# Attention bias by a plain load on the SP queue, masked by GpSimd additions, in place of a mask copy and an accumulating DMA

## What is computed

```python
scores = jnp.einsum('bhqd,bhkd->bhqk', q / math.sqrt(HEAD_DIM), k)
scores = scores + attention_bias
scores = jnp.where(src_mask, -jnp.inf, scores.astype(jnp.float32))
probs = jax.nn.softmax(scores, axis=-1).astype(v.dtype)
ctx = jnp.einsum('bhqk,bhkd->bhqd', probs, v)
```

## Time and profile before

| | |
|---|---|
| median of 3 runs | 686.55 us (685.88 to 686.61) |
| the profiled execution | 685.88 us, of which its span is 684.1 us |
| TensorE busy | 556.1 us, 81% |
| VectorE busy | 468.2 us, 68% |
| ScalarE busy | 296.7 us, 43% |
| GpSimd busy | 227.6 us, 33% |
| DMA | 86.50 MB, mean 126 GB/s |
| mean granted TensorE clock | 0.900 |

### The profile page before, as it was taken

The page is one execution under the profiler, slowest core; times in us unless marked ns, Lnnn a source line. Parts: engine busy times, 40 slices in busy tenths (PEclk is TensorE's granted clock), DMA queues, the critical chain, the costliest instruction groups (busy, mean ns, idle before and its releaser), DMA issues.

```text
span 684.1 us, 15743 instructions
## 1 busy us (share of the span) xinstructions
PE 556.1 (81%) x5032; PEld 415.9 (61%) x5033; DVE 468.2 (68%) x1300; ACT 296.7 (43%) x608; POOL 227.6 (33%) x137
## 2 busy tenths in 40 slices
PE   2719566999697998779948399999899999999992
PEld 0606255658385485764837248776676778777871
DVE  5574796589979979983798844886554656474751
ACT  1615542651564425525243141766564344353540
POOL 0412543207714338133280331212442223132222
PEclk9558768999989898979988689999999999999996
DMA  8583451913065452466606585782632322222220
GB/s 287 127 209 125 157 159 57 226 34 124 0 168 156 141 177 71 132 147 208 200 24 229 188 291 216 273 284 41 162 69 39 52 40 41 34 49 37 44 42 0
DMA packets 41177, 86.50 MB, mean 126 GB/s; under 512 B 7321, under 2 KB 31810, under 8 KB 37026
## 3 DMA queue, kind: packets, MB, share of 16 engines
q1 hardware_dynamic: 21744, 56.77, 24.3%
q0 software_dynamic: 8352, 16.99, 13.5%
q10 hardware_dynamic: 11026, 12.02, 5.9%
HBM read 57.23 MB, written 29.44 MB: 127 GB/s over the span
## 4 chain that ended last, share of the span: by engine, by line
PE 52%; DVE 25%; issue 6%; DMA 5%; ACT 5%; ACTq 3%; POOL 2%; SPq 0%; DVEq 0%; POOLq 0%
PE bank L1914 8%; PE bank L1903 5%; PE bank L1739 4%; PE bank L1905 4%; PE bank L1748 4%; PE bank L1904 4%; PE bank L1915 4%; DMA stage<-in_moe_w 4%; PE bank L1636 3%; PE bank L1703 3%; ACTq L850 2%; PE bank L1719 2%; PE bank L1654 2%; PE bank L1693 2%; DVE stats L1033 2%
## 5 line engine op out<-in xcount | busy, mean ns | idle before, releaser
L1903 PE MATMUL bank<-xs_f,w_moe 128*128 128x128 f16 x624 | 123.2, 221 | 13.0 <-ACT stage L862 6.0
L1905 PE MATMUL bank<-xs_f,w_moe 128*128 128x128 f16 x624 | 123.3, 221 | 0.0
L862 ACT ACTIVATE stage<-bank,cols 128x128 f32<-128x128 f32 x312 | 88.9, 374 | 78.7 <-PE bank L1905 35.2
L1904 PE MATMUL bank<-xs_f,w_moe 128*128 128x128 f16 x624 | 122.7, 220 | 0.0
L642 POOL DMA_INDIRECT out_x<-x_kept,ids x39 | 63.1, 1619 | 165.6 <-DVE x_kept L1505 102.3
L1903 PEld LDWEIGHTS bank<-xs_f,w_moe 128*128 x624 | 61.1, 98 | 49.9 <-issue 21.7
L1914 PE MATMUL bank<-w_moe,split 128*128 x208 | 79.3, 383 | 0.6
L1904 PEld LDWEIGHTS bank<-xs_f,w_moe 128*128 x624 | 61.4, 98 | 2.8
L1000 DVE SCALAR_TENSOR_TENSOR split<-stage,split 128x2048 f16<-128x2048 f32 x16 | 41.2, 2572 | 31.7 <-ACT split L681 31.7
L1739 PE MATMUL bank<-w_moe 128*128 128x512 f32 x128 | 59.8, 627 | 3.3 <-ACT w_moe L740 3.3
L1905 PEld LDWEIGHTS bank<-xs_f,w_moe 128*128 x624 | 61.2, 98 | 1.1 <-issue 0.2
(11 more groups left out here) (273 smaller groups left out, 1173.6 us busy)
## 6 DMA issues: line engine op xcount, KB each, us to landing
stage<-in_moe_w SPq DMA_DIRECT2D x16, 1024.0 KB, 8.6
w_split<-split SPq DMA_DIRECT2D x16, 1024.0 KB, 4.9
w_moe<-w_split SPq DMA_DIRECT2D x8, 2048.0 KB, 8.5
w_moe<-in_bias POOLq DMA_DIRECT2D x8, 1024.0 KB, 11.2
xs<-dispatched ACTq DMA_DIRECT2D x41, 130.0 KB
w_moe<-in_x_f SPq DMA_DIRECT2D x4, 512.0 KB, 6.8
w_moe<-in_x_t SPq DMA_DIRECT2D x4, 512.0 KB, 7.6
out_x<-x4b ACTq DMA_DIRECT2D x4, 512.0 KB, 3.6
```

Source lines behind the costliest of these rows:

```text
L862: ins = act.activation(h32[j][:, f, :], bank[banks + g][:, P * (f % 4):P * (f % 4) + P], ACT.Relu, bias=moe_b1[:, bass.ds(e, 1), f], scale ...
L1903: pe.matmul(o, hi, xs_f[j][:, k, :], start=(k == 0), stop=False)
L1904: pe.matmul(o, hi, xs_f[j][:, KD + k, :], start=False, stop=False)
L1905: mm = pe.matmul(o, lo, xs_f[j][:, k, :], start=False, stop=(k == KD - 1))
```

## The change

The bias no longer comes by an accumulating DMA on GpSimd's queue but by a plain load of the same 1 MB for each half, on SP's queue (`load_bias`). It waits only for the buffer to be free. The mask is no longer copied by ScalarE: GpSimd adds `mask_add` to the loaded bias in place, in four additions of 128x512 for each half, each of which VectorE waits for before it adds the scores of that part. The semaphore `mask_written` (one count a half) becomes `bias_masked` (four counts). GpSimd's `mask(c + 1)` stands behind `residual(c)`, ahead of `confirm(c)`; that of chunk 0 stands where `add_bias(0)` was. ScalarE's eight copies a chunk go.

```diff
@@ sync
+            def load_bias(c):
+                for u in range(2):
+                    sp.wait_ge(prob_turned[u].sem, prob_turned[u].of(c, 0))
+                    sp.dma_start(sc[u][:].rearrange("p r a h k -> p (r a h k)"),
+                                 t["bias"][bass.ds(c * 2 + u, 1), :, :].rearrange("s p n -> (s p) n")
+                                 ).then_inc(bias_in[u].sem, 16)
...
             load_x(0)
+            load_bias(0)
             load_x(1)
...
             load_tokens(2)
             for c in range(NCH - 1):
+                load_bias(c + 1)
                 store_part(c, 3)
                 load_part(c + 1, 0)
@@ gpsimd
-            def add_bias(c):
+            def mask(c):
                 for u in range(2):
-                    pool.wait_ge(mask_written[u].sem, mask_written[u].of(c, 1))
-                    pool.dma_start(sc[u][:].rearrange("p r a h k -> p (r a h k)"),
-                                   t["bias"][bass.ds(c * 2 + u, 1), :, :].rearrange("s p n -> (s p) n"),
-                                   accum_op=ALU.add).then_inc(bias_in[u].sem, 16)
+                    pool.wait_ge(bias_in[u].sem, bias_in[u].of(c, 16))
+                    for r in BANK_ORDER:
+                        pool.tensor_tensor(
+                            sc[u][:, r], sc[u][:, r],
+                            mask_add[:, bass.ds(c * TT + 2 * u, 2), :].unsqueeze(2).broadcast_to([P, 2, 4, S]),
+                            ALU.add).then_inc(bias_masked[u].sem, 1)
...
             pool.tensor_scalar(mask_add[:], mask_u8[:], MASKED, None, ALU.mult).then_inc(mask_ready, 1)
-            add_bias(0)
+            pool.wait_ge(mask_ready, 1)
+            mask(0)
...
             pool.wait_ge(main_in, N_MAIN)
-            add_bias(1)
             select(2)
             for c in range(NCH - 1):
                 residual(c)
+                mask(c + 1)
                 confirm(c)
                 less_maximum(c + 1, 0)
...
-                if c + 2 < NCH:
-                    add_bias(c + 2)
                 dispatch(c, range(TT))
@@ scalar
-            def mask(c, u):
-                act.wait_ge(prob_turned[u].sem, prob_turned[u].of(c, 0))
-                for r in range(4):
-                    ins = act.activation(sc[u][:, r],
-                                         mask_add[:, bass.ds(c * TT + 2 * u, 2), :].unsqueeze(2).broadcast_to([P, 2, 4, S]),
-                                         ACT.Copy)
-                ins.then_inc(mask_written[u].sem, 1)
...
             context(0, 0)
-            mask(1, 0)
             context(0, 1)
-            mask(1, 1)
             split_high(0, 3)
@@ vector
                         dve.wait_ge(score_done[u].sem, score_done[u].of(c, i + 1))
-                        if i == 0:
-                            dve.wait_ge(bias_in[u].sem, bias_in[u].of(c, 16))
+                        dve.wait_ge(bias_masked[u].sem, bias_masked[u].of(c, i + 1))
```

More of the change, by code:

```diff
@@ L351, in build @@
         v_done, v0_ready, v1_ready = free("v_done", 2), count("v0_ready", 2), count("v1_ready", 2)
-        mask_written = [count(f"mask_written{u}", 1) for u in range(2)]
+        bias_masked = [count(f"bias_masked{u}", 4) for u in range(2)]
         score_done = [count(f"score_done{u}", 4) for u in range(2)]
@@ L792, in _ @@
             act.activation(soft[:, 3], soft[:, 2], ACT.Ln).then_inc(setup_act, 1)
-            act.wait_ge(mask_ready, 1)
-            for u in range(2):
-                mask(0, u)
             act.wait_ge(main_in, N_MAIN)
@@ L835, in _ @@
                 context(c + 1, 1)
-                if c + 2 < NCH:
-                    for u in range(2):
-                        mask(c + 2, u)
                 split_high(c + 1, 2)
```

## The result

The changed kernel takes 699.63 us (median of 4 runs, 696.46 to 700.35), the kernel before 686.21 us beside it (685.84 to 686.61): ratio 1.0183, 95% interval 1.0164 to 1.0203. It is slower by 13.4 us; 9.25 were forecast.

A forecast was written before the change was run, and what follows sets the result against it. No engine was taken as the bound throughout; the chain in order of time was read. -2.1 + 0.9 + 2.05 + 5.6 + 2.8 = +9.25 on 686.55 gave 695.8 us; range 689 to 701, own case 692 to 699.

The forecast's parts named there:

- signs of being wrong: An addition of other than 1.0 us, Newton steps at 0.17 us throughout, or chunk 3's stage part landing in 8 us.
- Copies, -2.1: At 96.7 us, ScalarE's four mask copies ahead of `context(0, 1)` leave the chain: 2.1 us less.
- Chunk 0, +0.9: Additions run from 29.3 to 37.6 us; one falls under VectorE's Newton steps from 36.59 us: 0.9 us more.
- The stage load of chunk 0, +2.05: Near 50 us, an earlier stage part lets `split_low(0, 0)` between the two `shift_norm(0)` additions: 2.05 us more.
- Chunk 1, nothing: Additions at about 128 to 137 us run while VectorE idles or reads PSUM: no cost.
- Chunk 2, +5.6: Additions from 234.0 to 242.3 us hold seven of VectorE's nine Newton steps in chunk 3's norms: 5.6 us more.
- Chunk 3, +2.8: From 310.4 us chunk 3's bias on SP's queue delays the weight store and load behind it: 2.8 us more.
- the second pair starts 2.8 us later: `store_part(2, 3)` and `load_part(3, 0)`, issued at about 323 us, wait for 2 MB of bias moving at 280 GB/s until 326.2.
- hidden additions: Rival, chance 0.13: chunk 2's bias lands so that the norms are not hit; without the 5.6, 690.2 us.
- faster: Rival, chance 0.07: VectorE isn't held, the queue has room, the four copies at 96.7 us decide: -2.1 us, 684.5 us.
- Sharing: Rival, chance 0.10: the bias slows the weight part ahead of it, 7.3 instead of 2.8 us at 310 us: 700.3 us.
- A dear addition: Rival, chance 0.08: the broadcast makes each GpSimd addition cost 2 us instead of 1.04: 704 us.

The follow-up runs named there:

- again: The changed kernel measured and profiled a second time, no edit: 698.43 us, ratio 1.0187 to the kernel before.
- split0: The changed kernel, with VectorE made to wait for both additions of `shift_norm(0)` before `split_low(0, 0)`: 696.8 us, ratio 1.0163.
- noadd2: The changed kernel without the eight mask additions of chunk 2, loads as in the changed kernel: 689.9 us, ratio 1.0057.
- noadd: The changed kernel without any of the 32 mask additions, loads still on SP's queue: 685.13 us, ratio 0.9999.
- placed: The changed kernel with additions of chunks 0 and 2 moved, biases of chunks 2 and 3 loaded sooner, `split_low(0, 0)` behind both `shift_norm(0)` additions: 685.46 us, ratio 0.9993.
- bias3early: The changed kernel with chunk 3's bias loaded one weight part sooner, ahead of `store_part(2, 2)`: 700.88 us, ratio 1.0216.
- eight: The kernel before plus eight GpSimd additions of 128x512 into dead memory behind `residual(1)`, loads and copies untouched: 695.09 us, ratio 1.0133.
- maskmove: The kernel before with ScalarE's four mask copies `mask(1, 0)` moved behind `context(0, 1)`: 681.56 us, ratio 0.9933; second measurement 681.2 us, 0.9939.
- placed3: The kernel placed, with the second half of chunk 3's additions moved behind the weight part's `split_low(2, 3)`: 680.1 us, ratio 0.9932.

## Why the prediction was right or wrong

The direction was right, and the time, 699.63, lies within the range of 689 to 701, but it is 3.8 us above the forecast and outside the 692 to 699 that the prediction gave its own case. Two of its own signs of being wrong came: an addition took 1.26 us, and the stage part at chunk 3 landed in 8.00. Term by term, from the traces of after and again:

- **Copies, -2.1: right place, too small.** Measured 3.6 to 3.9 us in the changed kernel (from the maximum of (0,0) to `split_low(0,3)`: +3.3 to -0.6, +4.4 to +0.8). The chain's 2.07 us is only the idleness; the lower clock that this idleness left behind was another 1.5. The forecast never asked what TensorE's clock did behind a gap, although the 4.40 us of its 64 matmuls stood in the trace of before.
- **Chunk 0, +0.9: mechanism right, too small.** It was 2.0 us in after and in again (whose +2.4 at this point has 0.4 from before the additions). An addition takes 1.26 us instead of 1.04, so that the last ends at 39.1 instead of 37.6 us, and two steps are held instead of one (the next step starts at 40.35, before at 38.38).
- **The stage load of chunk 0, +2.05: right to the tenth.** 4.09 instead of 2.04 us for the pair, and split0 takes it away.
- **Chunk 1, nothing: right.** The additions run from 126.2 to 136.1 us in after; it is 0.6 us ahead of before at `split_low(0,3)` and 0.7 at the first scores of the chunk.
- **Chunk 2, +5.6: place, time and mechanism right, too small.** Its first half landed at 234.26 (234.0 forecast), and seven steps were held in after (seven forecast), eight in again. The landing was in part luck: the prediction let the halves follow each other at 272 GB/s, but from 230 us the engines moved 393 to 436 GB/s, and by 234.26 some 1.9 of the 2.1 MB were through (an estimate from the GB/s of each microsecond in after). The error is the price: 7 x (1.19 + 0.03 - 0.20) = 7.1 us, and `normalise`, which I had left out, 0.9 more. From `x4b` of chunk 0 to `split_low(1,3)` after lost 7.5 and again 6.8 us; a step that `residual(1)` held in before (L1019 at 225.64, 2.49 us) was held less (1.17 us in again), and gave 1.3 back. Without all of chunk 2's additions noadd2 is 8.5 us faster, net of what it loses in chunk 3.
- **Behind chunk 2, not in the forecast: +1.5.** At the transposes TensorE in before idled 2.04 us for VectorE's L1043 at 278 us, in again 4.59 us; then the clock was at its lower level, and eight matmuls took 1.97 instead of 1.09 us. The rows of before and of again:

```profile
271.57 4.33 PE L1703 MATMUL bank<-w_moe 128*32 128x64 f32 x64
277.95 1.09 PE L1601 MATMUL bank<-mats,w_moe 128*128 128x128 f32 x8 [2.04 <-DVE w_moe L1043]
```

```profile
278.39 3.18 PE L1697 MATMUL bank<-w_moe 128*32 128x64 f32 x64
286.16 1.97 PE L1595 MATMUL bank<-mats,w_moe 128*128 128x128 f32 x8 [4.59 <-DVE w_moe L1038]
```

It is not shown that the additions cause this. The longer idleness comes with TensorE having done the matmuls ahead sooner (3.18 instead of 4.33 us for the 64), and noadd, which has no additions and is 1.7 us ahead of before at `split_low(1,3)`, shows the same rows:

```profile
267.80 3.18 PE L1700 MATMUL bank<-w_moe 128*32 128x64 f32 x64
275.40 1.97 PE L1598 MATMUL bank<-mats,w_moe 128*128 128x128 f32 x8 [4.42 <-DVE w_moe L1041]
```

Over this stretch noadd loses 0.3 us, placed 0.5 and noadd2 0.8, all without additions over the Newton steps. How much of the 1.5 us is the additions' stays open.

- **Chunk 3, +2.8: the sum right by luck, the reason wrong.** Again lost 2.8 us from 306 to 338 us, but not through SP's queue. 1.6 of it is the slower first layer of `feed_forward`, at the lower clock; the other 1.2 the additions over `split_low(2, 3)` and the scores. The failed step is "the second pair starts 2.8 us later", and in it the rate: it took 280 GB/s from a stretch of before. That the 2 MB follow the part ahead held. In noadd2 the DMA engines moved 377 to 439 GB/s from 318 to 323 us and 8 GB/s in the microsecond behind, and the next pair, issued at 323.20 us, found them free. The bias fitted into the idle 4.3 us: the prediction's own lower bound, 0. So it was in again, with the bias issued at 320.12 us, the last of it moved by 333, and the next pair at 335.5. The other step that failed stood beside it: "the first additions end at 323.8 us, when scores want them", which looked at who waits for the additions and not at what runs under them. `split_low`, with two SBUF inputs, is such an instruction as L1019.

The sum from again: +2.4 (0.4 of it from the start) +2.05 -3.6 +0.6 (drift to 217 us) +6.8 +1.5 +2.8 +0.7 (tail) = 13.2, against the span's 13.2.

Of the rivals, **hidden additions** and **faster** fell: both needed the norms not to be hit. **Sharing** fell with noadd2, where the part ahead of the bias landed in 8.90 us against 8.89, and with bias3early, which loads the bias sooner and gains nothing. **A dear addition** came a quarter of the way: 1.26 between 1.04 and 2, and this alone is 1.1 us in chunk 0 and 1.3 in chunk 2. It should have been part of the likeliest case: the trace of before has GpSimd operations of 128x512 at 1.49 us (L580) and 1.61 us (L583) as rows for an upper price, beside the 0.91 and 3.09 us that the prediction named.

That VectorE's steps are held fits a rule of the Trainium skill (SBUF — State Buffer, "Who interferes with whom"): VectorE's second port pair is GpSimd's too, and an instruction that needs it while the other has it waits for the whole of that instruction. Most rows here agree (1.19 us for each addition of 1.26); the 12.11 us of eight go beyond it, since nine instructions passed there before one step.

What stays open: why `feed_forward`'s first layer at some 304 to 321 us starts at the lower clock in again, split0, bias3early and noadd (15.6 to 15.7 us), but not in before, eight, maskmove, noadd2, placed and placed3 (14.0 to 14.1 us), with gaps of 2.0 to 2.1 us right ahead of it in all of them. One thing goes with it. In the slow ones 64 matmuls ahead of it (L1654 of before, at 299 us) took 5.1 to 5.4 us instead of 6.0 to 6.5, and TensorE idled another 0.7 to 0.95 us before the eight transposes between them and the gap; in the others this second idleness is missing. No run changes it alone. Open too is why bias3early loses what it does behind 390 us.

## What to carry to other kernels

Work moved onto an idle GpSimd can be paid by VectorE: for every instruction of VectorE whose operands all lie in SBUF (here the statistics, and the row maxima with their one input, were not held), ask whether it will run under GpSimd's, and count one whole GpSimd instruction for each step of a chain of small ones. Where the additions stand decides more than how many there are: with the same 32 the kernel took 698.4 us or 680.1 us, by their places, four small waits and two bias loads issued sooner. And when a wait of TensorE of some 2 us goes or comes, look at how long the same matmuls take behind it at either clock; at the mask copies that was worth 1.5 us beside the 2.1 of the wait.

## What the runs showed of the hardware that was not expected

- A GpSimd addition with the second operand broadcast over a middle dimension took 1.26 us, against 1.04 for one of the same 128x512 size without it. Eight that read both inputs from another tile took 9.68 us (1.21 each).
- A VectorE step on four columns may be let in between each two GpSimd instructions (after, seven steps of 1.19 us) or not for nine of them in a row (eight, 12.11 us). What decides it no run shows. The cost of the eight additions was of one size both ways: 8.5 us without them in noadd2, 9.2 us with them in eight.
- The lower clock came with idleness that another engine caused: 2.47 us of it, ended at 99 us, were followed by 4.40 instead of 3.18 us for 64 matmuls.
- Two loads of 1 MB queued on SP behind a weight part slowed neither that part nor the next (noadd2: 8.90 against 8.89 us and 8.07 against 8.15).
- One profiled execution had VectorE stand still for 5.8 us with no engine or transfer waited for that the profile shows.
